# One attention-and-MLP kernel: V tiles of step 6 in other PSUM banks, pair 4's product ahead of the transposes, and one spread split 7/3/6

## The reference

```python
x = x + 0.5 * _L0_ffn_ref(_layernorm(x, axis=-1), L0_ffn_w1, L0_ffn_b1, L0_ffn_w2, L0_ffn_b2)
x = x + _L0_attn_ref(_layernorm(x, axis=-1), L0_attn_w_qkv, L0_attn_w_out, L0_attn_b_out)
x = x + 0.5 * _L0_ffn_ref(_layernorm(x, axis=-1), L0_ffn_w1, L0_ffn_b1, L0_ffn_w2, L0_ffn_b2)
```

## Time and profile before

| | before |
|---|---|
| median of 3 runs | 2157.73 us |
| lowest and highest | 2156.95, 2159.33 us |
| the profiled execution | 2157.49 us |
| its span in the trace | 2155.7 us |
| busy: PE, DVE, ACT, POOL | 2104.2, 1529.8, 1271.9, 1145.1 us |
| SP's issues of PT, POOL's | 1392, 646 |

### The profile page before, as it was taken

How to read it: one execution, slowest core, us unless ns; L and a number is a source line. 1 busy time by engine, 2 the same in 40 slices (tenths; PEclk the granted TensorE clock), 3 DMA queues, 4 the chain that set the end, 5 groups by cost and what they waited for, 6 DMA issues and landing times.

```text
span 2155.7 us, 42138 instructions
## 1 busy us (share of the span) xinstructions
PE 2104.2 (98%) x14480; PEld 1710.1 (79%) x14480; DVE 1529.8 (71%) x4121; ACT 1271.9 (59%) x3156; POOL 1145.1 (53%) x1988
## 2 busy tenths in 40 slices
PE   7999999999999999999999999999999999999997
PEld 6687787887878788787886878878787787877876
DVE  7776777767676776767767677676766777677674
ACT  5746656466564665756557465674646656565572
POOL 2754636546474563745547365473655637455461
PEclk9999999999999999999999999999999999999999
DMA  3433515234152341524425143251533415234142
GB/s 132 132 84 83 144 31 147 78 95 123 45 142 69 109 108 55 148 54 120 107 65 138 45 138 89 73 144 30 147 82 97 127 40 147 69 104 113 46 132 59
DMA packets 130294, 209.70 MB, mean 97 GB/s; under 512 B 42192, under 2 KB 70960, under 8 KB 130080
## 3 DMA queue, kind: packets, MB, share of 16 engines
q1 hardware_dynamic: 97888, 143.86, 23.6%
q0 software_dynamic: 25952, 58.38, 10.8%
q10 hardware_dynamic: 6240, 4.76, 0.8%
HBM read 14.95 MB, written 8.39 MB: 11 GB/s over the span
## 4 chain that ended last, share of the span: by engine, by line
PE 76%; DVE 9%; ACT 4%; POOL 4%; issue 3%; ACTq 2%; SPq 1%; DMA 1%; POOLq 0%; DVEq 0%
PE ps L361 75%; DVE P L945 3%; ACT P L711 2%; ACTq L301 2%; POOL P L1137 1%; POOL PT L290 1%; SPq L290 1%; DVE gl L836 1%; DVE P L937 1%; POOL rstd L1123 1%; DVE xs L868 1%; DVE st L844 1%; DMA PT<-P 1%; DVE x L884 1%; DVE gh L904 0%
## 5 line engine op out<-in xcount | busy, mean ns | idle before, releaser
L711 ACT ACTIVATE P<-P,mx 128x512 f32<-128x512 f32 (+3 forms) x1024 | 563.5, 553 | 271.3 <-DVE mx L937 271.1
L1137 POOL TENSOR_SCALAR P<-P,rs 128x512 f32<-128x512 f32 (+3 forms) x1024 | 540.1, 545 | 214.0 <-DVE rs L928 210.6
L290 POOL DMA_DIRECT2D PT<-P x646 | 325.1, 509 | 384.0 <-DVE P L945 357.2
L945 DVE STREAM_TRANSPOSE P<-P 128x1792 f32<-128x1792 f32 (+1 forms) x256 | 372.6, 1484 | 24.9 <-POOL P L1137 24.9
L361 PE MATMUL ps<-PT,v 128*64 128x256 f32 (+1 forms) x3072 | 306.6, 349 | 11.1 <-DMA PT<-P 9.8
L361 PE MATMUL ps<-qk 64*128 64x512 f32 (+3 forms) x2048 | 311.0, 443 | 0.7 <-ACT qk L657 0.7
L361 PE MATMUL ps<-w2h,gh 128*128 128x256 f32 x1024 | 291.9, 285 | 1.8 <-DVE gl L836 1.7
L361 PEld LDWEIGHTS ps<-PT,v 128*64 128x64 f32 x3072 | 204.1, 137 | 108.5 <-issue 17.4
L361 PE MATMUL ps<-w2l,gh 128*128 128x256 f32 x1024 | 289.7, 283 | 0.0
L361 PE MATMUL ps<-w2h,gl 128*128 128x256 f32 x1024 | 289.6, 283 | 0.0
L937 DVE CUSTOM_DVE_ANT_0 P<-ps,dist 128x512 f32<-128x512 f32 x256 | 166.1, 686 | 162.1 <-PE ps L361 161.6
(11 more groups left out here) (91 smaller groups left out, 4359.8 us busy)
## 6 DMA issues: line engine op xcount, KB each, us to landing
PT<-P SPq DMA_DIRECT2D x1392, 80.0 KB, 2.6
PT<-P POOLq DMA_DIRECT2D x646, 80.0 KB, 2.7
x<-in_L_attn_x SPq DMA_DIRECT2D x16, 512.0 KB, 4.4
out_y<-x SPq DMA_DIRECT2D x15, 512.0 KB, 2.9
xt<-xs SPq DMA_DIRECT2D x195, 32.0 KB, 2.1
xt<-xs POOLq DMA_DIRECT2D x165, 32.0 KB, 1.9
xt<-xs ACTq DMA_DIRECT2D x120, 32.0 KB, 2.2
raw<-in_L_ffn_w SPq DMA_DIRECT2D x2, 512.0 KB, 5.8
```

The lines of the kernel that those rows point to most:

```text
L290: e.dma_start(PT[c % 2][32 * m:32 * m + 32, g, :], P[c % 3][32 * g:32 * g + 32, m, :]).then_inc(landed.sem, 16)
L711: e.activation(p, p, ACT.Exp, bias=mx[:, r, i:i + 1], scale=-1.0, accum_out=sm[:, r, i:i + 1]).then_inc(s_ex.sem, 1)
L945: e.transpose(p, p).then_inc(s_tr.sem, 1)
L1137: e.tensor_scalar(p, p, rs[:, 2 * (c % 2) + h, i:i + 1], 1.0, ALU.mult, ALU.mult).then_inc(s_nz.sem, 1)
```

## The change

Four things are edited. In step 6 PE puts both V tiles into banks 0 and 1 and then goes on with banks 6 and 7, so that pair 4's product takes bank 6 and the first transposes bank 7. Pair 4's product stands ahead of the transposes instead of behind them. ACT copies that product out at the end of step 6, ahead of the rounding of the rows (`ln_hi`), instead of at the start of step 7. And the 16 DMAs of the second norm's spread are shared 7 by SP, 3 by ACT and 6 by POOL, as the third norm's are, instead of 6, 5 and 5. In the last batch only the bank edit applies.

```diff
-    X_SP = {2: GROUPS[:6], 3: GROUPS[:7]}
-    X_ACT = {2: GROUPS[6:11], 3: GROUPS[7:10]}
-    X_POOL = {2: GROUPS[11:], 3: GROUPS[10:]}
+    X_SP = {L: GROUPS[:7] for L in (2, 3)}
+    X_ACT = {L: GROUPS[7:10] for L in (2, 3)}
+    X_POOL = {L: GROUPS[10:] for L in (2, 3)}
...
-                    for tile in steps_v(b, c):
-                        proj_tile(b, tile)
+                    if c == NC - 2:
+                        among[0] = (0, 1)
+                        turn[0] = 1
+                        for tile in steps_v(b, c):
+                            proj_tile(b, tile)
+                        among[0] = (6, 7)
+                        turn[0] = 7
+                    else:
+                        for tile in steps_v(b, c):
+                            proj_tile(b, tile)
...
+                    if more or c < NC - 1:
+                        values(b, c - 2)
                     if more and c == NC - 2:
                         ln_transpose(1, b + 1, 0)
                         among[0] = (5,)
                         ln_transpose(1, b + 1, 1)
                         among[0] = (6, 7)
-                    if more or c < NC - 1:
-                        values(b, c - 2)
-                    if more and c == NC - 2:
                         turn[0] = 5
...
-                    if c >= 3:
+                    if c >= 3 and not (more and c == NC - 1):
                         out_copy(b, c - 3)
...
                     if more and c == NC - 2:
+                        out_copy(b, c - 2)
                         ln_hi(1, b + 1, 0)
                         ln_hi(1, b + 1, 1)
```

## The result

| | before | after |
|---|---|---|
| median | 2158.49 us (6 runs) | 2165.05 us (6 runs) |
| lowest and highest | 2156.95, 2160.11 us | 2163.84, 2168.58 us |
| ratio, 95% interval | | 1.0037, 1.0026 to 1.0047 |
| the profiled execution | 2157.49 us | 2164.67 us |
| its span | 2155.7 us | 2162.9 us |

The changed kernel is slower by 0.37%, 1.05 us more than the 2164.0 forecast. Busy PE is 98% as before.

The account below looks back on a forecast made before the run. PE, busy 98% of the span, was taken as the bound. Even batches -4.2, odd +9.2, batch 0 +0.5, moved pauses +4.5 and split -3.5 sum to +6.5 on 2157.49: 2164.0 us, range 2156.5 to 2169.5.

Parts of the forecast that it names:

- Odd batches, +1.32 each (+9.2): Later transposes delay roundings, low parts, turn and spread, so pair 6's product stalls 1.32 us in seven odd batches: +9.2 us.
- The spread's 8.8 us: Time assumed from SP's first issue of pair 6's spread DMAs to the start of pair 6's product.
- The third rival: Pair 6's product doesn't hang on the low part, so later rows are absorbed: 2139.8 us, chance 0.1.
- 245.7 in the old count: Batch 1: ACT's roundings forecast to start at about 245.70, when the copy-out ends, instead of 244.32.
- the 0.65 us of the earlier trace: Batch 1, pair 4: POOL was said to begin its issues 0.65 us after its releaser, without a pause.
- Even batches, -0.60 each (-4.2): Without POOL's pause on pair 4, seven even batches lose the 1.92 us stall and gain 1.32: -4.2 us in all.
- the moved pauses, +4.5: POOL's pauses move to pairs 3, 2 and 1; five batches wait 0.9 us each at products: +4.5 us.
- the 102: Spacing between POOL's paused issues, the first being its 129th; taken to stay with 52 issues a batch.
- The first rival: The pause stays on pair 4 of even batches, +0.5 us in each, split -3.5: 2167.2 us, chance 0.25.
- The split, -3.5: Fewer ACT issues of the second norm's spread free it for the last output rows PE waits for: 3.5 us gained.
- The bank edit, "at most 14.2 us": Ceiling on gain from ending the transposes' wait on the V copy, in seven even batches and batch 0.
- The 1.92 us of the earlier trace: Step 6's first V matmul to pair 6's product: 21.42 us in batch 2 against 19.50 in batch 1.

Follow-up runs that it names:

- e3: The changed kernel with the old 6/5/5 split of the second norm's spread; 2171.88 us, ratio 1.0064 to the kernel before.
- e12: The changed kernel with the same counts of GpSimd issues as e11; 2162.51 us, ratio 1.0026 to the kernel before.
- e11: e9 with GpSimd taking 3 issues of pair 4 and 4 of pair 5 instead of 4 and 3; 2141.39 us, ratio 0.9926 to the kernel before.
- e8: The changed kernel with pair 4's copy-out behind the two roundings of the rows instead of ahead; 2162.40 us, ratio 1.0021 to the kernel before.
- e2: The kernel before with the 7/3/6 split alone; 2150.59 us, ratio 0.9965 to the kernel before.
- e1: The kernel before with the bank edit alone; 2157.34 us, ratio 0.9998 to the kernel before.
- e5: The changed kernel with transposes back ahead of pair 4's product and copy-out back at step 7; 2152.93 us, ratio 0.9975 to the kernel before.
- e10: The kernel before with the 7/3/6 split and e9's 46 issues, without the bank edit; 2151.93 us, ratio 0.9973 to the kernel before.
- e4: The changed kernel with SP and POOL issuing 8 each of pair 6's spread and 14 and 2 of pair 7's; 2185.12 us, ratio 1.0126 to before.
- e9: e5 with 46 issues a batch on GpSimd instead of 52, the rest on SP; 2153.06 us, ratio 0.9980 to the kernel before.
- e6: e5 with 17 fewer PT issues on GpSimd in batches 0 and 1, moved to SP; 2150.29 us, ratio 0.9968 to the kernel before.

## Why the prediction was right, and where it was not

- **Odd batches, +1.32 each (+9.2): right.** Roundings, low parts and SP's first issue are 1.37 us later, as the chain said, S grows by 0.93 to 1.71 in the seven (median 1.35), +9.6 in all. The spread's 8.8 us, the assumption under it, were 8.96 and 8.79 us in the two batches shown, now with PE waiting for it. The third rival is dead by this: it needed under 7.5 us. Both other tests agree: odd batches of e3 against before (20.86, 19.52) and of e12 against e11 (20.96, 19.53).
- **Two readings were off without harm.** The sum took the roundings' start from the end of the copy (245.7 in the old count). e8 has no copy there and its roundings start at the same 5.97 us: PE's own order, with the transposes behind 2.3 us of product, sets them. And the 0.65 us of the earlier trace rows are POOL's idle time; it began 0.58 us after DVE's turn, its releaser, had ended.
- **Even batches, -0.60 each (-4.2), and the moved pauses, +4.5: the sum right by luck, the place wrong.** S of even batches changed by -0.9 us in all instead of -4.2, and nothing was lost at pairs 2 and 3. So the pause took 3.3 us (4.8 without the late landing of batch 8) in a place where none was forecast, and 4.5 were forecast where none was lost. The -0.60 of an even batch without a pause was right: e12 against before gives -0.54 in the six of them other than batch 8. Two steps failed. The first: the 102 was carried over to 52 issues in a batch ("the same numbers fall on pair 3 in batches 2 and 4, pair 2 in 6, 8 and 10, pair 1 in 12 and 14"). The spacing is 104 then (and 92 with 46, 87 where two batches had 87), so the pause doesn't wander over pairs 3, 2 and 1, but stays on pair 3 of every even batch. The second: the price of a pause was read at the products alone. On pair 3 it was put at nothing, because pair 4's product has room, and that product did not wait. (On pairs 1 and 2 it never fell, so what it costs there no run shows.) What it delayed was POOL's normalising, DVE's turn of pair 4 and ACT's exponentials of step 6, by 0.4 us less than before, and the copy ahead of the roundings takes that 0.4 back (e8). Hence 21.45 against 21.42.
- **The first rival** had the mechanism of the even batches (late exponentials, +0.5 each) and the pause tied to its surroundings. The pause did move, and the even batches lost nothing, though its 2167.2 lies only 2.2 us off. Its +0.5 is right where the pause does stay on pair 4: e3 has it there, and S of its even batches is 21.92 against 21.43.
- **The split, -3.5: right, somewhat more.** -5.7 in the output projection and +1.4 behind it; e2 gave -4.7 and +1.3. The ol waits went as the row of ACT's issues said.
- **The bank edit, "at most 14.2 us": right as a ceiling, and it gave nothing (e1, e5, e10).** The 1.92 us of the earlier trace rows can be had, but from the pause's place: e11 has them in all seven batches (-13.6 us).
- **Not in the sum:** +0.9 us ahead of the first step 6 and +1.35 behind the last. In the other kernels these two ranged from -0.3 to +2.0 and from -0.6 to +1.8, so I take them as scatter between executions, which was not tested. That 2164.0 lies within 1.1 us of the median is in part luck: the even batches with their pauses came out 1.2 us under their terms and the split 0.8 under, and these two made 2.25 us that no term had.

## What to carry to other kernels

A stall in the bounding engine is worth what the next constraint leaves: follow each engine behind it (here ACT's exponentials, and from the low part over the turn to the spread) before a wait is priced at its length. Work put ahead of the head of a long chain is paid in all that exceeds the chain's slack: here the transposes came 2.40 us later, 1.0 us of that was slack ahead of the roundings, and 1.4 us arrived at pair 6's product. Where a pause or a queue's delay recurs, change where it falls before changing what waits for it; and moving an issue from one queue to another moves everything behind it there (e4, e9).

## What the runs showed of the hardware

**POOL's DMA issues pause once in two batches.** In every kernel the stream stops ahead of its 129th issue. Between two issues of one pair the gap is 2.17 or 2.33 us; ahead of a pair's first issue it is 3.14 us, against 0.65 us without a pause (5.41 us in e6, of which 2.7 stand behind the end of DVE's turn). The paused issues after it are 230 (before, e3), 232 (after, e2, e5), 215 (e6), 220 (e9, e11, e12), which is 128 plus the issues of batches 0 and 1 (102, 104, 87, 92, counted up to batch 1's third norm) each time, and they repeat at the number of issues of two batches. What the count restarts from, and what POOL does in the pause, no run shows. The rule of the Trainium skill that I had weighed ("SBUF — State Buffer", section "SBUF: two separate sides") is not its cause: the pause left the place beside DVE's row normalising as soon as the counts changed.

**The same section bears on something else here.** It says that of a GpSimd operation and a VectorE operation in a mode that takes both ports, or with two inputs in SBUF, the one that starts first holds the shared port pair for its whole length and blocks the other. In which mode the row normalising runs, no trace shows. e11 looks like such a lock: counted from the start of the row normalising, DVE's last three operations end at 1.09, 1.79 and 2.38 us, each 0.15 us after one of POOL's (0.94, 1.64, 2.23). e9 fits it only in part: there the second operation began at 0.30 us, ahead of POOL's at 0.62, and yet took 2.03 us, past the ends of two of POOL's (1.32, 1.98). Why this alignment costs 1.6 us stays open. Shown is that POOL's normalising starts 0.4 us earlier in e11 (0.19 us after the row normalising, against 0.62), and that S is some 0.6 us shorter and the whole about 0.55% faster (e9 against e11).
